# VectorE makes layer 2's four column sums itself, in a two-layer convolution kernel on one core

## The reference

```python
def _gn(v, G=16, eps=1e-05):
    g = v.reshape(B_, G, C_ // G, H_, W_)
    m = jnp.mean(g, axis=(2, 3, 4), keepdims=True)
    s = jnp.var(g, axis=(2, 3, 4), keepdims=True)
    return ((g - m) / jnp.sqrt(s + eps)).reshape(v.shape)

x = x + _L0_conv_ref(_gn(x), L0_conv_weight, L0_conv_bias)
x = x + _L1_conv_ref(_gn(x), L1_conv_weight)
```

## Time and profile before

| | us |
|---|---|
| median of 3 runs (331.82 to 332.74) | 331.9 |
| the profiled execution's own time | 331.95 |
| its span | 329.9 |
| TensorE busy (matmuls) | 269.3 |
| VectorE busy | 281.0 |
| ScalarE busy | 151.9 |
| GpSimd busy | 137.3 |

### The profile page before, as it was taken

One profiled execution on the slowest core, in us unless ns is written; L12 is line 12 of the kernel. 1 busy time (PEld: TensorE's weight loads), 2 busy tenths in 40 slices (PEclk: granted clock), 3 DMA queues, 4 the chain that ended last, 5 costly groups with the idle time before them and its releaser, 6 DMA issues.

```text
span 329.9 us, 5435 instructions
## 1 busy us (share of the span) xinstructions
PE 269.3 (82%) x1572; PEld 159.2 (48%) x1572; DVE 281.0 (85%) x555; ACT 151.9 (46%) x328; POOL 137.3 (42%) x127
## 2 busy tenths in 40 slices
PE   0032985968959739999999999999999999999691
PEld 0032543534635315656665666566556655665350
DVE  3999999797999799977996899689968996577994
ACT  3451374477924544462746263645364153523230
POOL 3626000900961357125723491439053903540730
PEclk9997895899998969999999999999999999999987
DMA  7645000003301004321412141221023003302015
GB/s 83 92 86 86 7 2 1 0 0 89 63 0 54 26 2 84 63 78 29 84 30 78 38 85 20 78 48 24 0 78 74 0 2 87 66 0 78 0 40 105
DMA packets 62690, 15.31 MB, mean 46 GB/s; under 512 B 61521, under 2 KB 61649, under 8 KB 62673
## 3 DMA queue, kind: packets, MB, share of 16 engines
q1 hardware_dynamic: 58848, 14.70, 22.0%
q10 hardware_dynamic: 3824, 0.41, 1.0%
HBM read 5.27 MB, written 4.72 MB: 30 GB/s over the span
## 4 chain that ended last, share of the span: by engine, by line
DVE 42%; PE 30%; issue 11%; ACT 7%; DMA 3%; SPq 3%; POOL 1%; DVEq 1%; ACTq 0%; POOLq 0%
PE banks L1230 29%; DVE lo L683 6%; DVE wl L583 3%; DVE X L713 3%; DVE s L662 3%; DMA Z<-X 3%; DVE wl L552 2%; DVE gt L517 2%; ACT junk L914 2%; DVE s L676 2%; DVE X L745 2%; DVE s L674 2%; POOL X L1148 1%; SPq L332 1%; ACT wh L973 1%
## 5 line engine op out<-in xcount | busy, mean ns | idle before, releaser
L1230 PE MATMUL banks<-hi,wh 128*128 128x384 f16 (+3 forms) x504 | 100.9, 340 | 20.7 <-ACT hi L951 7.9
L1230 PE MATMUL banks<-lo,wh 128*128 128x384 f16 (+3 forms) x504 | 99.0, 335 | 2.0 <-DVE lo L683 1.9
L1230 PE MATMUL banks<-hi,wl 128*128 128x384 f16 (+3 forms) x504 | 97.5, 332 | 0.0
L1148 POOL TENSOR_TENSOR X<-X,ps 128x384 f32 (+1 forms) x31 | 38.6, 1244 | 129.7 <-DVE ps L697 74.4
L319 POOL TENSOR_TENSOR pre<-P 128x442 f32<-128x442 f32 (+3 forms) x59 | 63.2, 1102 | 45.8 <-ACT P L943 32.0
L1230 PEld LDWEIGHTS banks<-hi,wh 128*128 128x128 f16 x504 | 50.3, 102 | 55.7 <-issue 16.7
L951 ACT CAST hi<-s 128x384 f16<-128x384 f32 (+3 forms) x80 | 40.1, 537 | 68.2 <-DVE s L672 38.3
L1230 PEld LDWEIGHTS banks<-lo,wh 128*128 128x128 f16 x504 | 50.1, 100 | 38.7 <-DVE lo L683 3.4
L1230 PEld LDWEIGHTS banks<-hi,wl 128*128 128x128 f16 x504 | 49.8, 99 | 34.8 <-issue 1.6
L683 DVE TENSOR_TENSOR lo<-s,hi 128x384 f16<-128x384 f32 (+3 forms) x80 | 51.6, 668 | 0.9 <-ACT hi L951 0.8
L914 ACT ACTIVATE junk<-X 128x576 bf16 (+1 forms) x62 | 42.3, 682 | 16.5 <-DVE X L745 10.7
(11 more groups left out here) (123 smaller groups left out, 238.9 us busy)
## 6 DMA issues: line engine op xcount, KB each, us to landing
X<-in_x SPq DMA_DIRECT2D x64, 72.0 KB, 2.6
out<-X SPq DMA_DIRECT2D x60, 72.0 KB, 2.3
Z<-X SPq DMA_DIRECT2D x8, 432.0 KB, 3.9
Z<-X SPq DMA_DIRECT2D x8, 144.0 KB, 3.6
Z<-X SPq DMA_DIRECT2D x32, 12.0 KB, 2.3
stage<-in_w SPq DMA_DIRECT2D x4, 100.0 KB, 3.7
out<-X ACTq DMA_DIRECT2D x4, 72.0 KB, 2.9
tab<-in_tables ACTq DMA_DIRECT2D x1, 86.0 KB, 4.0
```

Of the source, the lines that this page charges most:

```text
L1148: tt(cols(n, v), cols(n, v), src[c][:, :], ALU.add).then_inc(res_done[c], 1)
L1230: ins = nc.tensor.matmul(dst[:, o0:o1, u0:u1], wbuf[c][:, j, at:at + P], xbuf[c][:, j, i0:i1, g + u0:g + u1], start=(part == 0 and i == 0) ...
```

## The change

`streams_ahead` is called for layer 2 alone, for pairs 0 to 6. It now calls `own_stream`, which exists already and is used at the start of layer 1 and for one stream of the last pair: VectorE makes the sum and then the stream that uses it. GpSimd's call of `pre_sums(2, n - 1)` goes. GpSimd keeps layer 1's sums, the residual adds of both layers, and three sums of the last pair. The semaphores count as before.

```diff
             def streams_ahead(c, n):
 
                 stream3(c, n)
-                make_stream(c, n, 0)
-                make_stream(c, n, 1)
+                own_stream(c, n, 0)
+                own_stream(c, n, 1)
                 low_half(c, n, 0)
-                make_stream(c, n, 2)
+                own_stream(c, n, 2)
                 low_half(c, n, 1)
-                make_stream(c, n, 3)
+                own_stream(c, n, 3)
...
                 if prep and not first and not early:
                     pre_sums(1, n + 1)
-                if not first and not last:
-                    pre_sums(2, n - 1)
                 if not last and not early:
                     residual(1, n)
```

## The result

The changed kernel takes 341.98 us (median of four runs, 340.66 to 342.21), the kernel before, run beside it, 332.32 (331.82 to 332.86). The ratio is 1.0287 with an interval of [1.0271, 1.0303]: slower, by 9.7 us. The profiled execution took 342.07 us with a span of 340.1, against 331.95 and 329.9, so the traces differ by 10.1 us. The forecast was 340.3 (336.6 to 342.7): the median lies inside that range, but above the 339 to 341.2 to which the prediction gave 60 in 100.

The account below looks back on a forecast made before the run. The prediction took VectorE's chain, 32.12 us a step with TensorE about 0.4 behind, as the bound. Its terms, 3.1 + 5.6 - 0.3 = 8.4 us on 331.95, gave 340.3, range 336.6 to 342.7.

Parts of the forecast that it names:

- second step, to TensorE's restart: First layer 2 streams, at 94 us: 3.1 us of sums added, less lengthening given back, +0.9, shifting TensorE's restart at 121.20.
- loop step 2, to the next L697: Three lengthened operations stand before and after, so all four sums on VectorE are extra: +3.1 us.
- loop steps 3, 4, 5: Each grows by 3.1 - 4.2 + 2.5 = 1.4 us; with step 6, 5.6 us, and nothing hides it.
- step 6 and the last layer 2 block but one: Step 6 grows by 1.4 us; in the block at 283 us, 3.1 goes and 3.1 comes, so nothing.
- last L745 of layer 1: Near the end L745 waits 0.29 us for TensorE; VectorE's delay eats that: -0.3.
- L697 stays within 0.3 of 128.24. The 0.9 is gone.: Loop step 2: GpSimd's old sums go, VectorE gets back over 0.9 us, cancelling the second step's delay.
- A clock rival: TensorE's clock falls as idle time before the statistics matmul grows to 1.9 us a step: 341.1 to 342.7; 15 in 100.
- "2.5 us" for three stretched operations: VectorE's block behind L697: the early residual adds lengthen three operations, costing 2.5 us where five cost 4.2 before.
- an own sum: One layer 2 sum made on VectorE costs 0.78 us, wait included; four a step are 3.1 us.
- the shared time falls, so nothing is lost: All four GpSimd sums lengthened VectorE's chain by 0.92 us, so a step changes by -0.6: 332.3 us; 5 in 100.
- The rival of the stricter lock: Each lengthened operation loses a whole GpSimd operation, 1.1 us; step grows 0.9; with the half case 336.5 to 338.5, 15 in 100.
- The rival "faster": Early residual adds lie beside L697, L698 and VectorE's waits, costing nothing: 330.9 us; 3 in 100.

Follow-up runs that it names:

- The filled kernel: The changed kernel with 22 unread matmuls on TensorE ahead of layer 1's second stream in step 2: 340.02 us, ratio 1.0227.
- the table of seven kernels: L697 to L703 times of seven kernels against sums on VectorE and operations lengthened by GpSimd: 9.68 us (sums only removed) to 14.34 (only added).
- the kernel with two moved: The changed kernel with GpSimd making the first two layer 2 sums again, VectorE only the third and fourth: 334.23 us, ratio 1.0064.
- the kernel without adds: The changed kernel with GpSimd's layer 1 residual adds cut to one column from pair 2 on: 331.71 us, ratio 0.9984.
- the kernel before with filled matmuls: The kernel before with 22 unread matmuls ahead of the second stream of layer 1's pair 2: 333.05 us, ratio 1.0017.
- the kernel with both the split wait and the filling: The kernel before with L713's wait for GpSimd's residual adds split in two, and the 22 unread matmuls: 331.52 us, ratio 0.9983.

## Why the forecast held, and where it was off

By the start marks of the two traces (before, after, and the shift added in the part):

| part | forecast | measured |
|---|---|---|
| second step, to TensorE's restart: 121.20, 122.04 | +0.9 | +0.84 |
| restart to L697 of loop step 2: 128.24, 129.41 | -0.9 | +0.33 |
| loop step 2, to the next L697: 158.97, 163.16 | +3.1 | +3.02 |
| loop steps 3, 4, 5, to 196.94, 230.73, 264.12 | +1.4 each | +1.61, +1.64, +1.61 |
| step 6 and the last layer 2 block but one, to L697 at 292.32, 302.77 | +1.4 + 0 | +1.40 |
| last L745 of layer 1: 298.76, 308.85 | -0.3 | -0.36 |
| sum | 8.4 | 10.1 |

The sum of 8.4 was 1.7 too low in these two traces. Two steps were off: one by its reason, which brings 1.2, and one by its size, 0.6.

*"L697 stays within 0.3 of 128.24. The 0.9 is gone."* This step failed. VectorE did get its time back there, as said, but L697 then waited 2.70 us for TensorE, whose matmuls behind the restart ran longer at 1.2 GHz than before (until about 128 against 125), though the idle time ahead of them was shorter (5.15 us against the 6.21 of the earlier trace rows). L697 moved by 1.17 instead of 0. The step was wrong in its size too: VectorE got back 2.4 us, where "over 0.9" was forecast (from the restart to L697 less its wait are 4.67 us, 7.04 before). The filled kernel shows the cause: at full clock the wait is gone, and L697, less the 0.77 by which that execution started later, would stand at 126.7, 1.5 us earlier than before. So 128.24 fits neither clock; that the forecast lies between the two is luck. A clock rival stood in the prediction, with 341.1 to 342.7, and 341.98 lies in it; but it was laid at another place, the idle time of every step that grows from 0.4 to 1.9. That idle time came (1.54 + 0.42 us), in nearly the size foretold, and the clock stayed at 1.00 through the step. What should have been asked is what the step where TensorE had just restarted, already at its lower clock, does when VectorE's cover over it goes. Six of the ten runs of the changed kernel took 1.2 us less, 340.5 to 341.0; if the difference lies at this restart, as is likely, L697 was near its forecast place in them. No trace shows it.

*"2.5 us" for three stretched operations.* This term was mis-sized by 0.2. The third in the row is the own sum L319. From its start at 200.95 to L672 at 202.78 are 1.83 us, where an own sum alone has 0.78: 1.05 lost. I had priced the third as L672's 0.80, from the earlier trace rows. 3.1 - 4.2 + 2.7 = 1.6, as measured, and the three steps bring 0.6 us. Its own row has 1.70, where the prediction's list of signs had 1.4. Why it loses more than L672 did is not shown. That three are stretched, which three, and that the first add comes 1 us after L697 were right, and the table of seven kernels shows the sum's parts one by one.

Right as priced: an own sum (from start to start 0.82 at 203.31 in the loop, 0.78 in the earlier trace rows, so the wait on a register's value costs 0.04 at most, inside the 0.1 that was allowed), the second step's 0.9, loop step 2's four bare sums at 3.0, and the last block, where a wait of 0.85 and three stretched operations went and four sums came. There, 8.61 us from 283.71 to 292.32 became 8.60 from 294.17 to 302.77. TensorE's last wait went too: L745 follows its own engine now.

```profile
308.85 0.73 DVE L745 SCALAR_TENSOR_TENSOR X<-banks,tab,X 128x384 f32<-128x384 f32 x1
```

The rival that "the shared time falls, so nothing is lost" is nearly true of two sums in four in loop steps 3 to 5, as the kernel with two moved shows, and false of the other two, for the reason that the prediction gave. The rival of the stricter lock, with the Trainium skill's rule ("SBUF — State Buffer", section "Who interferes with whom") taken at a full GpSimd operation per stretched one, would have had a step at 0.9; 1.61 was measured, and 0.85 is what one costs in the table. That operations with two SBUF inputs contend with a reading GpSimd is as that section says in this block of each of these traces, and L697 and L698, with one such input, keep their 0.6. Two inputs are not the only case: L633, a two-column operation with one input that takes 0.17 alone, took 0.89 at 118.01 in the changed kernel beside GpSimd's sums. The prediction's reason for the smaller loss, that a waiting operation is partly under way, no run tests. The rival "faster" needed the adds to lie beside work that they don't stretch; without any adds the block was 2.7 us shorter, so they cost all of the 2.5 that was forecast for them and a little more.

## What to carry to other kernels

Where two engines take turns at memory, work moved from one to the other is priced by where it lay: beside a wait or beside operations that don't contend it was free, and moving it costs its whole length; beside contending operations each one gives one stretch back. Count them one by one in the row, over the stretch that is on the path, and price the operation that will be stretched, not the one that was. And when VectorE's work goes from over a stretch in which TensorE has just restarted, look at the granted clock there, since the matmuls behind it may be next.

## What the runs showed of the hardware that was not expected

- The two engines' turns are not always one for one. In the kernel without adds, GpSimd's first one-column add took 0.19 us and the second 1.57. The second began at 161.84, 0.02 us before VectorE's L662, and ended when L662 and L319 were through; GpSimd's timeline of loop step 3:

```profile
161.29 0.19 POOL L1149 TENSOR_TENSOR X<-X,ps 128x1 f32 x1 [7.11 <-DVE ps L697]
161.84 1.57 POOL L1149 TENSOR_TENSOR X<-X,pd 128x1 f32 x1 [0.36 <-DVE pd L698]
```

- TensorE's clock did not fall for idle times of 1.54 and 0.42 us in each loop step (1.00 from 176.5 to 211). In the idle time of 5.15 us it stayed at 1.00 for 4 us and fell 1 us before its end, and the matmuls behind it ran at 0.50 for nearly 6 us; in the longer idle time of the kernel before, 6.21 us, it fell 3 us before the end, and the matmuls behind it had 1.00 again 4 us after the restart. A longer idle time was the cheaper one here.
- The same kernel took 341.9 to 342.3 us at a mean clock of 0.943 or 0.944 in four of its ten runs, and 340.5 to 341.0 at 0.952 to 0.957 in six. What decides it is open.
- The time of an execution beside its span is 2.0 us in most runs (342.07 and 340.1), but was 2.9 to 3.2 in eight of twelve runs of the kernel before with filled matmuls, at an unchanged span, and 3.2 and 3.5 in two of twelve of the kernel with both the split wait and the filling. A median of times can move by that alone.
